# Causal attention: the mask of the by-query scores added inside the vector engine's maximum instead of by a matrix product

## What is computed

```python
h = _rmsnorm(x, ln1_w)                       # x: 64 x 249 x 64 (T = 249 tokens)
q = (h @ wq.T) ...                           # 4 heads of 16 channels; k, v: 2 heads, each used twice
q = q * cos + _rotate_half(q) * sin
k = k * cos + _rotate_half(k) * sin
scores = jnp.einsum('bhtd,bhsd->bhts', q, k) / jnp.sqrt(jnp.float32(HD))
causal = jnp.tril(jnp.ones((Tx, Tx), dtype=bool))
scores = jnp.where(causal[None, None], scores, jnp.float32(-1e+30))
att = jax.nn.softmax(scores, axis=-1)
y = jnp.einsum('bhts,bhsd->bhtd', att, v) ...
x = x + y @ wo.T
flat = _rmsnorm(x, ln2_w)                    # and the router's top-2 shares, for the next stage
```

## Time and profile before

| | |
|---|---|
| median of 3 runs | 4983.44 us (4972.28 to 4985.36) |
| the profiled execution | 4976.66 us, of which the span from first to last instruction is 4974.9 us |
| busy over the span | PE 87%, PEld 59%, VectorE 57%, ScalarE 47%, GpSimd 42% |
| granted clock of TensorE, mean of the span | 0.887 of full speed |
| the groups of this stage, 1320 to 1800 us | PE busy 440.6 of 480 us, VectorE 304.0, clock 0.92 |

### The profile page before, as it was taken

How to read it: one execution, slowest core, us unless ns; L and a number is a source line. 1 busy time by engine, 2 the same in 40 slices (tenths; PEclk the granted TensorE clock), 3 DMA queues, 4 the chain that set the end, 5 groups by cost and what they waited for, 6 DMA issues and landing times. The chain is left out here.

```text
span 4974.9 us, 112547 instructions
## 1 busy us (share of the span) xinstructions
PE 4307.4 (87%) x32465; PEld 2931.3 (59%) x32465; DVE 2816.8 (57%) x7945; ACT 2333.3 (47%) x5965; POOL 2091.0 (42%) x2436
## 2 busy tenths in 40 slices
PE   7599947576999996999966576999999999799999
PEld 6377623464666664666656443566666666466665
DVE  3467625453566653444434465777777777455554
ACT  5355524211333333444422232677777777455555
POOL 0133337553344432222157564455555555333333
PEclk9999966796899997999955566999999999899999
DMA  1111123221011103333311122000000000133332
GB/s 44 38 28 28 25 46 99 62 56 34 21 26 27 25 23 77 79 79 79 70 35 42 43 52 47 9 9 9 12 9 10 11 9 11 37 72 72 77 71 58
DMA packets 483067, 206.67 MB, mean 42 GB/s; under 512 B 452472, under 2 KB 473198, under 8 KB 482802
## 3 DMA queue, kind: packets, MB, share of 16 engines
q1 hardware_dynamic: 482930, 204.98, 18.2%
HBM read 158.99 MB, written 45.91 MB: 41 GB/s over the span
## 5 line engine op out<-in xcount | busy, mean ns | idle before, releaser
L3366 POOL TENSOR_TENSOR att_P<-att_P,att_rden 125x498 f32<-125x498 f32 x512 | 520.3, 1017 | 564.8 <-DVE att_rden L3659 564.8
L3553 ACT ACTIVATE att_P<-att_pS,att_nb 125x249 f32<-125x249 f32 x1024 | 471.3, 474 | 0.3 <-DVE att_nb L3667 0.3
L2654 DVE TENSOR_TENSOR moe_hT<-moe_silu,moe_pH 128x498 f32<-128x498 f32 x384 | 258.8, 674 | 326.4 <-ACT moe_silu L2640 326.4
L3988 ACT ACTIVATE sw_hT<-sw_pH,sw_b 128x498 f32<-128x498 f32 x512 | 317.8, 672 | 242.8 <-PE sw_pH L3942 242.8
L3560 ACT ACTIVATE att_PTr<-att_pP 125x498 f32<-125x498 f32 x512 | 303.2, 592 | 156.0 <-PE att_pP L3476 148.5
L3476 PEld LDWEIGHTS att_pP<-att_ident,att_P 124*125 124x125 f32 (+1 forms) x2048 | 262.5, 187 | 184.7 <-issue 184.7
L3667 DVE TENSOR_REDUCE att_nb<-att_pS 125x2 f32<-125x498 f32 x512 | 323.2, 668 | 84.7 <-PE att_pS L3464 83.1
L2640 ACT ACTIVATE moe_silu<-moe_pH 128x498 f32<-128x498 f32 x384 | 225.1, 586 | 286.6 <-PE moe_pH L2597 200.7
L3476 PE MATMUL att_pP<-att_ident,att_P 124*125 124x124 f32 (+1 forms) x2048 | 353.1, 295 | 6.0 <-POOL att_P L3366 2.4
L3852 POOL TENSOR_TENSOR sw_acc<-sw_acc,sw_Z 128x249 f32<-128x249 f32 x224 | 154.8, 691 | 386.1 <-DVE sw_Z L4062 385.3
L2573 POOL TENSOR_TENSOR moe_xe<-moe_share,moe_x 128x1992 f32<-128x1992 f32 x32 | 130.0, 4063 | 444.4 <-DMA moe_share<-mixing 426.8
(11 more groups left out here) (467 smaller groups left out, 10721.5 us busy)
## 6 DMA issues: line engine op xcount, KB each, us to landing
moe_share<-mixing SPq DMA_DIRECT2D x64, 498.0 KB
sw_share<-mixing SPq DMA_DIRECT2D x64, 498.0 KB
ffn_W<-in_ffn_pairs SPq DMA_DIRECT2D x64, 192.0 KB
att_F<-h_stream SPq DMA_DIRECT2D x192, 62.5 KB
att_X<-h_stream SPq DMA_DIRECT2D x192, 62.5 KB
h_stream<-att_H SPq DMA_DIRECT2D x64, 62.5 KB
ffn_F<-h_stream SPq DMA_DIRECT2D x64, 62.5 KB
ret_F<-h_stream SPq DMA_DIRECT2D x64, 62.5 KB
```

Source lines behind the costliest of these rows:

```text
L2654: v.tensor_tensor(hT[:, u, k, :, :], sl[:, k % 3, :, :], pH[:, k % 3, :, T:2 * T], ALU.mult).then_inc(*hid_ready.one())
L3366: g.tensor_tensor(own, own, bc(rden[:, j % 2, c, :], T), ALU.mult).then_inc(*scaled.one())
L3553: ins = a.activation(P[:, r, c, t, :], pS[:, 2 * r + c, t * T:(t + 1) * T], ACT.Exp, bias=nb[:, r, c, t:t + 1], accum_out=den[:, r, c, t:t ...
L3988: a.activation(hT[:, k % 4, :, :], pH[:, place, :, 0:T], ACT.Relu, bias=b1[:, k:k + 1]).then_inc(*hid_ready.one())
```

## The change

The product that fills the by-query bank with the mask is dropped. `query_bank` keeps only its wait. The scores' products by query now start their bank anew (`start=True`). The vector engine adds the mask itself: each `tensor_reduce` becomes a `tensor_tensor_reduce`, which adds the float32 mask from SBUF to the scores from PSUM, multiplies by -1, writes the 125 or 249 results to a new SBUF tile `scores`, and keeps the smallest of them (starting from 2e30), which is minus the largest masked score. Because `scores` has two buffers, a wait for the maximum of step s - 2 is added on the vector engine, together with one semaphore increment (`st.held`). `mask16` keeps only the mask by key.

```diff
-        mask16 = st.sb("mask16", [PT, 2, LOW], BF16)
+        mask16 = st.sb("mask16", [PT, LOW], BF16)
+        scores = st.sb("scores", [PT, 2, LOW])
...
-                def mask_query(n, s):
+                def query_bank(n, s):
                     pe.wait_ge(*max_ready.after(n, s - 2))
-                    pe.matmul(pS[:, 2 + s % 2, 0:LOW], ident16[0:PT, 0:PT], mask16[:, 0, :], start=True, stop=True)
...
-                    pe.matmul(pS[:, s % 2, 0:LOW], ident16[0:PT, 0:PT], mask16[:, 1, :], start=True, stop=True)
+                    pe.matmul(pS[:, s % 2, 0:LOW], ident16[0:PT, 0:PT], mask16[:, :], start=True, stop=True)
...
                     return pe.matmul(pS[:, 2 + s % 2, out], qT[r:r + ROOM, u % 2, b, q], kT[r:r + ROOM, u, b, k],
-                                     start=False, stop=True, tile_position=(r, 0), skip_group_check=True)
+                                     start=True, stop=True, tile_position=(r, 0))
...
-                    mask_query(n, step)
+                    query_bank(n, step)
...
-                v.tensor_copy(mask16[:, :, :], mask[:, :, :])
+                v.tensor_copy(mask16[:, :], mask[:, 1, :])
...
                     v.wait_ge(*s_done.after(n, step))
-                    v.tensor_reduce(M[:, 0, b, hd, D:DV], bank[:, 0:PT], AX.X, ALU.max, negate=True)
-                    v.tensor_reduce(M[:, 1, b, hd, D:DV], bank[:, PT:LOW], AX.X, ALU.max, negate=True).then_inc(
-                        *max_ready.one())
+                    v.wait_ge(*max_ready.after(n, step - 2))
+                    st.held(v)
+                    v.tensor_tensor_reduce(scores[:, step % 2, 0:PT], bank[:, 0:PT], mask[:, 0, 0:PT], -1.0, -2.0 * NEG, ALU.add,
+                                           ALU.min, M[:, 0, b, hd, D:DV])
+                    v.tensor_tensor_reduce(scores[:, step % 2, PT:LOW], bank[:, PT:LOW], mask[:, 0, PT:LOW], -1.0, -2.0 * NEG,
+                                           ALU.add, ALU.min, M[:, 1, b, hd, D:DV]).then_inc(*max_ready.one())
```

## The result

Times are medians, with the ratio to the kernel before as it ran on the same chip in the same job, and its 95% interval. The medians are over all runs, while the ratios leave out any run more than 1.5% above the fastest of its kernel: here that of 5057.2 us, and two runs each of r1 and r2 further down.

A forecast was written before the change was run, and what follows sets the result against it. PE was taken to bound the stage, with gaps. 29 groups at 0.84 us plus 7.2 us for the slow start gave 31.6 us saved: 4945 from the profiled execution, 4952 from the median, given as 4950 us, range 4932 to 4988.

The forecast's parts named there:

- The sum: Whole touched stage: 29 groups at 0.84 us plus 7.2 us at its slow start, 31.6 us saved; forecast's chance 0.60.
- the slow first stretch: Stage's first 82 us, at 1.2 GHz: 24 dropped products at 0.30 us each save 7.2 us.
- a wait for `of`: PE's wait ahead of the transpose of `of`: grows from 0.65 to 0.81 us, so step 3 gains nothing.
- step 7: Last step of a group: scores start at once, gaining 0.30 - 0.10 = 0.20 us; wait for the maximum near 0.8 us.
- The third rival: Vector engine's new operation at its upper price, 0.75 us a step: 4980 us, no change; chance 0.10.
- the first rival: Longer PE waits lower the clock and take the gain back: 4983 us, no change; chance 0.20.
- one more slow stretch in each group: Waits of 2.2 instead of 1.7 us add one 1.2 GHz stretch of 1.1 us, so a group loses 0.26 us.
- the two clock rivals: Lower clock from longer PE waits takes back the gain (4983 us, chance 0.20) or makes it slower (5015 us, 0.10).
- The second rival: Clock falls behind each of a group's three waits, two more times a group: 32 us more, 5015 us; chance 0.10.
- a slow PE waits less: Argument against the clock falling behind all three waits: at 1.2 GHz PE idles less; no size given.
- The prediction's sign about the first slow stretch: Forecast would be wrong if the stage's slow start ended a group earlier or later (0.30 against 0.16 us a product).
- Two instructions a step became four: Vector engine's added operation, reading, increment and wait in each step: 0.10 us a step.

The follow-up runs named there:

- r1: Kernel after, with 112 semaphore increments nobody waits for put into the vector engine's program ahead of attention 1's loop: 5010.8 us, ratio 1.0044.
- r2: Kernel after, with 112 semaphore increments nobody waits for at the start of the stage behind the touched one: 4989.1 us, ratio 1.0003.
- b1: Kernel before, its three waits a group filled with 2, 4 and 4 repeated by-key mask products: 4939.0 us, ratio 0.9906.
- r5: Kernel after, with 112 idle increments ahead of the loop and its three waits filled with 5, 5 and 4 repeated by-key mask products: 4906.6 us, ratio 0.9865.
- r7: Kernel before without the by-query mask product, old maximum kept, plus one 125-column vector-engine copy a group ahead of step 5's maximum: 4996.0 us, ratio 1.0027.
- e2: Kernel before with the by-query mask product left out and the old maximum kept, so that mask is missing: 4926.8 us, ratio 0.9885.
- r3: Kernel before, with 40 semaphore increments nobody waits for at the start of the stage behind the touched one: 5007.1 us, ratio 1.0037.
- e4: Kernel after, its three waits a group filled with 5, 5 and 4 repeated by-key mask products, no padding: 4958.7 us, ratio 0.9944.

## Why the prediction was wrong

**The sum was right, for a clock that holds.** It said 31.6 us, and b1 against r5 gives 32.4, all in attention 1 (697.7 - 665.6 = 32.1). A turn is 2.92 us shorter, 0.73 a group where 0.84 was forecast; 29 groups give 21 us, and the other 11 lie ahead of the first transpose of `of`, 8.7 us (7.2 forecast for the slow first stretch), and at the end. That the total comes so close is partly luck, since these two differences cancel. Its working holds too: steps of 0.25 us instead of 0.41, a wait for `of` of 0.79 us (11.1 / 14; 0.8 forecast), step 7 at 0.90 (0.8), operations of 0.289 and 0.413 us. The third rival is out. The prediction's words "by that rule the sum would be the one of the third rival" don't follow from "the new operation has one SBUF source", just ahead of them. The 19.37 us of the earlier trace rows is the longest group of a turn and the 18.18 after one of the shortest, so their difference overstates the gain.

**The step that failed is the first rival's price of the clock**: "one more slow stretch in each group", each at 1.1 us. It saw the right danger, waits of 2.2 us a group instead of 1.7, and counted stretches, all as long as those before. There were fewer after, and what changed was how long each lasted: 3.4 us before, up to 61.4 after. At that length one of them costs more than the group gains: the group of 29.59 us is 11.4 longer than one of 18.18. Even a short one was priced low: a turn of four groups with one each takes 81.9 us before, and 76.3 without them in b1, a difference of 1.4 a group. The 0.30 that I gave the two clock rivals rested on that price. The forecast itself gave the clock no term. The second rival had the right sign, but counted in the same way. The argument "a slow PE waits less" is true and didn't help: in the stretch shown at 1.2 GHz PE is busy 58.7 of 60 us, and the clock doesn't come back in it. The prediction's sign about the first slow stretch came as well: it lasted 78.5 us instead of 116.1, and up to the first transpose of `of` the profiled execution after gained 13.9 us. The next 28 groups lost 47.3.

The Trainium skill, page "TensorE: Matmul & The Clock Gate", section "A second HAM failure mode: psum-queue depth-cycling", speaks of throughput lost to re-throttling and re-warming where the matrix engine idles briefly between groups of matmuls. The runs agree (r7 against e2: 0.13 us more waiting a group, 69 us), so I had weighed it too lightly.

**One term was missing.** "Two instructions a step became four" was priced at 0.10 us a step, as time of the engine, and not as code. It moved a loop of another stage so that it is loaded in every turn, 19.1 us in attention 3, shown by r3 from before and by r1 and r2 from after. No step of the prediction read q14's line on the page before (68 packets). Without these loads the time is still no gain: r1 5010.8 us (ratio 1.0044), r2 4989.1 (1.0003).

The Trainium skill, page "Runtime: NRT & Kernel Launch", section "Instruction fetch mechanics", says that an engine's small instruction memory is refilled in blocks of 16 KiB, and that a taken branch whose target isn't held has to wait for a load. The trace agrees with the wait (2.8 to 3.1 us, once a turn). It doesn't bear out the size: here a packet is 8.2 KB, and five are loaded in a turn.

**The account of +13.0 us**: +19.1 for attention 3; the touched stage -6, where -32 was there to be had. The clock took the other 26. By the means, 25.2 us, the touched stage is at +6 and the clock took 38. Such a remainder comes from runs that vary by 80 us with the clock: r1 and r2, with the same work in the stage, give +26 and +4 for it by their medians. In the touched stage the load of code costs something too once the waits are filled: e4 and r5 differ only in 112 increments, and attention 1 takes 700.6 us in the one and 665.6 in the other. With the waits open, r1 shows no such gain. What makes one stretch last 3.4 us and another 61.4 stays open: the runs show that waits lengthen them, not by what rule.

## What to carry to other kernels

Where a kernel waits at the edge of the clock, price work taken from TensorE twice: as time, and as idle time that may hold the clock down. Put something into the waits (here products that are overwritten) before judging such a change. When an edit lengthens an engine's loop, compare the packets of the instruction queue before and after, and look for "issue" waits once a turn in every stage behind it: 40 instructions of padding decided about 20 us here.

## What was unexpected of the hardware

- The lengths of the stretches at 1.2 GHz come in a few sizes, mostly 3.4, 13.7, 17.1, 27.3, 30.7 and 61.4 us between the stage's first stretch and its last; one copy of 0.22 us a group changed which of them appear.
- A vector engine's loop of 347 instructions ran 13 turns without a load or with five packets in each, by its place alone: 73.9 or 75.3 us a turn. One of 365 did the same (q14 160 after, 71 in r1).
- The accumulating operation with one operand from PSUM and one from SBUF was as fast as the plain addition of the earlier trace rows: 413 against 417 ns at 249 columns.
